# Query sets of one batch, key sets of two batches, and the last two query sets turned on GpSimd

## The chip, the cores and the metric

The kernel runs on one core of one Trainium2 chip. Its engines are TensorE (PE), VectorE (DVE), ScalarE (ACT), GpSimd (POOL) and SyncE (SP), which issues nearly all DMAs. The metric is the time of one execution on the device, in microseconds. The kernel before took 234.39 us (median of three runs, 233.6 to 234.4).

## The reference

One transformer block on x of 4 batches, 256 tokens, 512 features, in float32:

```
h  = layernorm(x)
q  = rope(h @ wq)   # 32 heads of 16
k  = rope(h @ wk)   # 8 key heads of 16, each serves 4 query heads
v  = h @ wv
a  = softmax(causal(q k^T / 4)) v
x  = x + layernorm(a @ wo)
z  = layernorm(x)
y  = z @ W_base^T + b + 16/16 * sum_e route_e(z) * B_e (A_e z)   # 8 experts, top 2
out = x + layernorm(y)
```

rope takes the pairs (re, im) of a head's features and gives re*cos - im*sin and re*sin + im*cos, with tables over the 256 positions.

## The kernel before

**Input.** Eight tiles of 128 tokens are loaded, normalised on DVE (`input_norm`), turned on PE (`turn_x`) and copied by ACT to `xn_t`, features on partitions (`copy_xnt`). SP issues the loads in program order (L298 to L314), and they travel in that order: x0, identity, wv, x1 to x3, half of wq, x4 to x7, tables, wk, the other half of wq, then the mask and the late weights.

**Projection sets.** Queries and keys are projected in float32 in five sets (L264): (half of the tokens, half of the heads) for queries, and one set "K" with all tokens. A set is 8 matmuls of 128x512 for queries. K is 16 matmuls of 64 columns of weights that run in pairs. Each set fills two PSUM banks, one for re and one for im.

**Rope and split.** Four products on DVE (L820), then the re half on DVE and the im half on POOL. Each half is split into three bf16 parts (high, middle, low) whose sum is the float32 value: ACT casts the high and middle parts (L606, L616), DVE (L831, L837) or POOL (L466, L470) subtract. The parts are written to DRAM (`write_q`, `write_k`) and loaded back (`load_q`, `load_k`), with heads apart and parts stacked on 96 partitions: one group is one batch and 4 key heads (16 query heads), and there are 8 groups. Queries lie in a ring of 5 slots `qst`, keys in a ring of 5 slots `kst`.

**The main loop.** There are 45 steps; unit n is one key head of one batch, 32 units in all. PE's step n does `scores(n)` (L1085, L1089; one bank), `scores_t(n-9)` (L1131), `scores_more(n)` (L1100, L1105; two banks), a piece of projection in steps 0 to 4 (L1036), `turn_max` at step 6, 10, ... (L1114) and, from step 14, a third of `attend` (L1146). DVE takes maxima of the scores (L964, L967), which frees their banks for the next step; every fourth step it splits the maxima in two bf16 parts (L977, L978). ACT copies the turned maxima (L726), SP stacks them under the queries (`stack_max`, L376), and `scores_t` then gives scores minus maximum, turned, which ACT exponentiates (L716, L719). POOL masks them (L543), and `attend` multiplies with the values. Sums and their inverses go through DRAM (`send_out`, `store_rden`, `spread_rden`).

**The fifth set** (i = 4) is the late one: 3 of its 8 matmuls run before the loop, 5 in steps 0 to 4. ACT copies its two banks to SBUF at step 5 (L746), POOL does the four products (L478) and both halves (L482), and `split_high`, `leave_late` (step 10), `split_middle`, `low_late` (step 12) and `write_q(4)` (step 14) follow. All engines work through their queues in program order, and every cross-engine dependence is a semaphore. After the loop the rest (output projection, layernorms, experts) runs in tiles of 128 tokens (`tile_step`), and the change doesn't touch it.

What must hold before the first scores is in `scores` and what PE runs before is in these lines:

```
            turn_and_project_v(0)
            project(0)
            turn_and_project_v(4)
            for i in range(1, 4):
                project(i)
            project(4, 0, 2 * KC - sum(MATMULS_4))
```

## Time and profile before

| what | us |
|---|---|
| median of three timed runs | 234.39 |
| the profiled execution's own time | 235.09 |
| its span, first to last instruction | 233.4 |
| PE busy (matmul) | 201.3 (86%) |
| DVE busy | 173.3 (74%) |
| ACT busy | 125.6 (54%) |
| POOL busy | 113.2 (49%) |

The span is cut into four stages below: until about 54.4 us the inputs are normalised and projected, from there the loop's steps 0 to 8 run until about 74.5, steps 9 to 13 until 88.8, and then PE is busy nearly all the time. A busy PE isn't a PE at its peak, since the ends of pipelined matmuls are modelled; idle time before an instruction and what ended it stand in brackets in the timeline.

### The profile page before, as it was taken

Reading aid. Unit: us, or ns where it says so; the run is one execution under the profiler, and the core shown is the slowest. Engines: PE = TensorE matmul, PEld = TensorE weight load, DVE = VectorE, ACT = ScalarE, POOL = GpSimd, SP = SyncE. Lnnn points to the kernel's source line nnn. Section 1 sums busy time; section 2 is a strip of 40 time slices with the busy share of each in tenths; the row PEclk is TensorE's granted clock in tenths of the full one; section 3 lists DMA queues with packets and bytes.
Section 4 is the critical chain, followed back from the end, with each engine's and each line's share of the span. In section 5 each row is a group of like instructions: output and inputs, shape, how many; then the busy total and the mean of one; then the engine's idle time right before and its main releaser. Section 6 shows DMA issues by size and latency. Waiting matters only on the chain.

```text
span 233.4 us, 3763 instructions
## 1 busy us (share of the span) xinstructions
PE 201.3 (86%) x1292; PEld 123.5 (53%) x1304; DVE 173.3 (74%) x364; ACT 125.6 (54%) x222; POOL 113.2 (49%) x96
## 2 busy tenths in 40 slices
PE   0499999999787879999999989899889989998860
PEld 0394843444454544444444524144778868997830
DVE  1773525767998897868696884686798898888785
ACT  3231440341214877888766785773577488773321
POOL 8200231562439695798743446462746262433352
PEclk9999999999999999999999999999999999999985
DMA  5998048976996302696673203344330001110113
GB/s 162 383 367 328 0 138 164 233 200 168 202 220 144 66 1 76 165 181 125 143 143 65 48 11 51 101 90 95 51 93 0 3 0 45 46 48 0 45 45 135
DMA packets 22465, 26.73 MB, mean 115 GB/s; under 512 B 3760, under 2 KB 17328, under 8 KB 21680
## 3 DMA queue, kind: packets, MB, share of 16 engines
q1 hardware_dynamic: 22304, 26.38, 44.8%
q8 instruction: 10, 0.16, 0.3%
q10 hardware_dynamic: 144, 0.13, 0.2%
q14 instruction: 7, 0.06, 0.1%
HBM read 17.19 MB, written 6.95 MB: 103 GB/s over the span
## 4 chain that ended last, share of the span: by engine, by line
PE 48%; DVE 22%; ACT 10%; issue 9%; DMA 5%; POOL 3%; SPq 2%; DVEq 0%; POOLq 0%
PE ps L1146 7%; PE ps L1194 7%; PE ps L1131 6%; PE ps L1105 4%; PE ps L1046 4%; PE ps L1169 4%; DVE stats L772 4%; PE ps L1036 3%; DVE nmax L967 3%; PE ps L1022 3%; DVE nmax L964 2%; ACT L577 2%; ACT region_a L719 2%; DMA x_sb<-x 2%; PE ps L1085 2%
## 5 line engine op out<-in xcount | busy, mean ns | idle before, releaser
L543 POOL TENSOR_SCALAR_AFFINE_SELECT region_a<-region_a 128x1024 f32<-128x1024 f32 x32 | 36.9, 1154 | 26.9 <-ACT region_a L719 26.7
L967 DVE TENSOR_REDUCE nmax<-ps 128x4 f32<-128x1024 f32 x32 | 39.1, 1223 | 10.3 <-PE ps L1105 10.0
L719 ACT ACTIVATE region_a<-ps 128x1024 f32<-128x1024 f32 x32 | 32.7, 1022 | 0.2 <-PE ps L1131 0.2
L1036 PE MATMUL ps<-region_a,region_c 128*128 128x512 f32 x64 | 29.0, 598 | 0.0
L1131 PE MATMUL ps<-region_b,kst 98*128 98x512 bf16 x96 | 26.8, 381 | 1.6 <-ACT region_a L719 1.1
L716 ACT ACTIVATE region_a<-ps 128x512 f32<-128x512 f32 x32 | 19.2, 599 | 16.4 <-PE ps L1131 15.9
L964 DVE TENSOR_REDUCE nmax<-ps 128x4 f32<-128x512 f32 x32 | 21.8, 682 | 4.8 <-PE ps L1089 4.4
L1146 PE MATMUL ps<-region_a,v_aug 128*32 128x512 f32 x192 | 25.3, 603 | 0.0
L583 ACT ACTIVATE std<-mv,eps_sb 128x1 f32<-128x1 f32 x32 | 9.3, 293 | 22.4 <-DVE mv L773 22.3
L1105 PE MATMUL ps<-kst,region_b 96*128 96x128 bf16 x256 | 19.6, 219 | 1.4 <-DVE nmax L967 0.8
L462 POOL TENSOR_TENSOR region_a<-region_a 128x512 f32<-128x512 f32 x4 | 6.5, 1627 | 28.9 <-DVE region_a L820 28.9
L1105 PEld LDWEIGHTS ps<-kst,region_b 96*128 96x128 bf16 x256 | 17.0, 98 | 5.5
L535 POOL TENSOR_TENSOR x_sb<-x_sb,region_b 128x512 f32<-128x512 f32 x8 | 10.2, 1278 | 18.9 <-ACT region_b L646 18.9
L530 POOL TENSOR_TENSOR region_b<-x_sb,region_b 128x512 f32<-128x512 f32 x7 | 9.0, 1281 | 19.4 <-ACT region_b L646 19.4
L1036 PEld LDWEIGHTS ps<-region_a,region_c 128*128 128x128 f32 x64 | 11.6, 190 | 12.8 <-issue 12.8
L820 DVE TENSOR_TENSOR region_a<-ps,region_c 128x512 f32<-128x512 f32 x16 | 9.9, 684 | 10.4 <-PE ps L1022 5.4
L772 DVE BATCH_NORM_STATS2 stats<-x_sb 128x6 f32<-128x512 f32 x16 | 11.0, 688 | 7.2 <-DMA x_sb<-x 6.1
L1194 PE MATMUL ps<-wcat_h,xn_h 128*128 128x324 f32 x64 | 11.6, 323 | 3.8 <-ACT xn_h L659 3.8
L577 ACT ACT_TABLE_LOAD x11 | 14.1, 1283 | 1.0 <-PEq L1290 0.8
L606 ACT CAST region_c<-region_a 128x512 bf16<-128x512 f32 x8 | 4.8, 618 | 18.3 <-DVE region_a L828 17.3
L1131 PEld LDWEIGHTS ps<-region_b,kst 98*128 98x128 bf16 x96 | 7.6, 97 | 12.3 <-ACT region_a L719 3.4
L1089 PE MATMUL ps<-kst,region_b 96*128 96x128 bf16 x128 | 12.4, 219 | 1.8 <-ACT mrow L726 0.8
(107 smaller groups left out, 415.3 us busy)
## 6 DMA issues: line engine op xcount, KB each, us to landing
q_scr<-region_c SPq DMA_DIRECT2D x24, 128.0 KB, 2.6
region_b<-q_scr SPq DMA_DIRECT2D x8, 384.0 KB, 5.2
x_sb<-x SPq DMA_DIRECT2D x8, 256.0 KB, 5.7
region_b<-q_scr SPq DMA_DIRECT2D x8, 256.0 KB, 5.6
attn_t<-o_sb SPq DMA_DIRECT2D x32, 64.0 KB, 2.4
rden_bc<-r_scr SPq DMA_DIRECT2D x8, 256.0 KB, 3.4
out<-region_b SPq DMA_DIRECT2D x7, 256.0 KB, 2.0
kst<-k_scr SPq DMA_DIRECT2D x8, 192.0 KB, 3.5
```

The lines of the kernel that those rows point to most:

```text
L543: pool.affine_select(out=blocks, in_=blocks, compare_op=ALU.is_ge, fill=0.0, base=0, pattern=[[0, 2], [0, REP], [1, P]], channel_multiplie ...
L577: nc.scalar.activation(unused[:, k, t:t + 1], eps_sb[:, 0:1], (ACT.Exp, ACT.Sqrt)[k])
L716: nc.scalar.activation(probs[:, u % PRING, 0, :], ps[:, 3, :], ACT.Exp, scale=float(HEAD_DIM) ** -0.5).then_inc(exp_done, 1)
L719: nc.scalar.activation(probs[:, u % PRING, 1:3, :], ps[:, 4:6, :], ACT.Exp, scale=float(HEAD_DIM) ** -0.5).then_inc(exp_done, 1)
L772: link(nc.vector.bn_stats(stats[:, k, t, :], src))
L964: nc.vector.tensor_reduce(nmax[:, gi % 2, 0, heads], ps[:, 0, :].rearrange("p (r k) -> p r k", r=REP), AX.X, ALU.max, negate=True).then_in ...
L967: nc.vector.tensor_reduce(nmax[:, gi % 2, 1, heads], ps[:, 1:3, :].rearrange("p a (r k) -> p r a k", r=REP), AX.XY, ALU.max, negate=True). ...
L1036: last = nc.tensor.matmul(ps[:, SET_BANKS[i][ri], :], wq_sb[:, c, col:col + P], xn_t[:, c, half * HALF:(half + 1) * HALF], start=(c == 0), ...
L1105: last = nc.tensor.matmul(ps[:, 1 + kt, r * P:(r + 1) * P], qst[0:SROWS, slot, h, P:2 * P], kst[0:SROWS, slot, k, kt * P:(kt + 1) * P], st ...
L1131: last = nc.tensor.matmul(ps[:, 3 + j, :], kst[0:TROWS, slot, k, kt * P:(kt + 1) * P], qst[0:TROWS, slot, k * REP:(k + 1) * REP, qt * P:(q ...
L1146: last = nc.tensor.matmul(ps[32 * j:32 * j + 32, 6 + qt, :], v_aug[:, 2 * b + kt, g * GROUP_KV + j, :], probs[:, u % PRING, qt + kt, :], s ...
L1194: last = nc.tensor.matmul(ps[:, 4 + 2 * (t % 2) + hf, 0:CATH], act_part[:, t % 2, c, :], w[:, c, hf * CATH:(hf + 1) * CATH], start=(term = ...
```

## The change

Query sets become one batch each with all 32 heads: 16 matmuls of 128x256. Key sets become two batches each: 16 matmuls of 64 columns by 256, in pairs. The six sets are q0, k01, q1, k23, q2, q3 (`SETS`). The first three are projected before the loop with their rope on DVE, both halves; k23 is projected last before the loop, and its rope is done on DVE in steps 0 to 3. Sets q2 and q3 are projected in steps 0 to 7, four matmuls in each, into banks 6 and 7; ACT copies them to SBUF (`LATE_COPY`), and POOL does all of their rope and subtractions (`LATE_ROTATE`, `LATE_HIGH`, `LATE_MIDDLE`). Before the loop POOL now does nothing but clear memory. The loads go x0, identity, x1, all of wq, x2, x3, tables, wk, x4 to x7, wv. Keys are written once for each part and repeated by the load (`load_k`, three DMAs with a broadcast source), and a ring of three whole batches holds them. The slots of `probs` are numbered from 3 (`slot_of`, `FIRST_SLOT`). The maxima's mask tile gives its place to `den_pk` and `rden_pk`, and `nmr` has two of four rows.

The diff, cut to its core ("..." marks what is left out):

```diff
-LOADS = {7: 4, 15: 5, 18: 6, 22: 7}
+LOADS_Q = {9: 4, 15: 5, 18: 6, 22: 7}
+LOADS_K = {8: 2, 18: 3}
 VECTOR_OUT = 5
@@ -69,10 +72,14 @@
 POWER_TILE = 5
-ROPE_3 = {0: 1, 1: 2}
-MATMULS_4 = (1, 1, 1, 1, 1)
-ROTATE_4, SPLIT_HIGH_4, SPLIT_MIDDLE_4, WRITE_4 = 5, 10, 12, 14
+LATE_PROJECT = 4
+K_ROPE = {0: 0, 1: 1, 2: 2, 3: 3}
+K_HIGH, K_MIDDLE = 2, 3
+LATE_COPY = {2: (2, 0), 4: (2, 1), 6: (3, 0), 8: (3, 1)}
+LATE_ROTATE = {2: 0, 8: 1}
+LATE_HIGH = {6: 4, 10: 5}
+LATE_MIDDLE = {7: 4, 12: 5}
+LATE_WRITE = {7: 2, 14: 3}
...
-        SETS = [(0, 0), "K", (0, 1), (1, 0), (1, 1)]
-        SET_BANKS = [(2, 3), (4, 5), (6, 7), (2, 3), (4, 5)]
-        set_of = {s: i for i, s in enumerate(SETS)}
-        WRITES_Q, WRITES_K = 16 * 2 * PARTS, 16 * 2 * len(RUNS)
-        LOADS_QK = 16 * (len(RUNS) + 1)
+        SETS = [("q", 0), ("k", 0), ("q", 1), ("k", 1), ("q", 2), ("q", 3)]
+        SET_BANKS = [(2, 3), (4, 5), (2, 3), (4, 5), (6, 7), (6, 7)]
+        DIRECT = 4
+        WRITES = 16 * 2 * PARTS
+        LOADS_OF_ONE = 16 * len(RUNS)
...
             sp.dma_start(ident_sb[:, :], ident).then_inc(ident_loaded, 16)
+            sp.dma_start(x_sb[:, 1, :], x[P:2 * P, :]).then_inc(x_loaded[1], 16)
+            sp.dma_start(wq_sb[:, :, :], wq.rearrange("(c p) n -> p c n", p=P)).then_inc(wq_loaded, 16)
+            for t in range(2, TILES):
+                sp.dma_start(x_sb[:, t, :], x[t * P:(t + 1) * P, :]).then_inc(x_loaded[t], 16)
+                if t == 3:
+                    sp.dma_start(tab_sb[:, :, :], tables).then_inc(tab_loaded, 16)
+                    sp.dma_start(wk_sb[:, :, :], wk.rearrange("(c p) n -> p c n", p=P)).then_inc(wk_loaded, 16)
             sp.dma_start(wv_sb[:, :, :], wv.rearrange("(c p) n -> p c n", p=P)).then_inc(wv_loaded, 16)
-            wq_v = wq.rearrange("(c p) n -> p c n", p=P)
-            for t in range(1, TILES):
-                if t == 4:
-                    sp.dma_start(wq_sb[:, :, 0:256], wq_v[:, :, 0:256]).then_inc(wq_loaded[0], 16)
-                sp.dma_start(x_sb[:, t, :], x[t * P:(t + 1) * P, :]).then_inc(x_loaded[t], 16)
-            sp.dma_start(tab_sb[:, :, :], tables).then_inc(tab_loaded, 16)
-            sp.dma_start(wk_sb[:, :, :], wk.rearrange("(c p) n -> p c n", p=P)).then_inc(wk_loaded, 16)
-            sp.dma_start(wq_sb[:, :, 256:512], wq_v[:, :, 256:512]).then_inc(wq_loaded[1], 16)
...
+            def load_k(b):
+                sp.wait_ge(k_written[b], WRITES)
+                if b >= KRING:
+                    sp.wait_ge(t_psum, 2 * KV_HEADS * (b - KRING + 1))
+                for part, (first, count) in enumerate(RUNS):
+                    rows = k_scr[b, part].rearrange("i f h n -> (i f) (h n)")
+                    sp.dma_start(kst[first * HEAD_DIM:(first + count) * HEAD_DIM, b % KRING, :, :],
+                                 rows.unsqueeze(0).broadcast_to([count, HEAD_DIM, KV_HEADS * SEQ]))\
+                        .then_inc(k_loaded[b % KRING], 16)
...
             write_q(0)
+            write_k(0, (0, 1))
             load_q(0)
+            write_k(0, (2,))
+            load_k(0)
+            load_q(1)
+            write_k(1, range(PARTS))
+            write_q(1)
+            load_k(1)
             load_q(2)
-            for part in range(PARTS):
-                for half in range(2):
-                    write_k(part, half)
-            load_k(0)
-            load_k(1)
-            write_q(2)
-            load_q(1)
-            load_k(2)
-            load_k(3)
             load_q(3)
-            write_q(3)
+            write_k(2, range(PARTS))
+            write_k(3, range(PARTS))
             for n in range(MAX_LAG, STEPS + 5):
...
+                if n in LATE_WRITE:
+                    write_q(LATE_WRITE[n])
+                if n in LOADS_K:
+                    load_k(LOADS_K[n])
+                if n in LOADS_Q:
+                    load_q(LOADS_Q[n])
...
+            def rotate_late(j):
+                cos, sin = (tab_sb[:, k, :].unsqueeze(1).broadcast_to([P, 2, SEQ]) for k in range(2))
+                re, im = (late_set[:, i, :].rearrange("p (g n) -> p g n", g=2) for i in range(2))
+                pool.wait_ge(tab_loaded, 16)
+                if j:
+                    pool.wait_ge(late_low, 2 * j)
+                for m, val, table in ((0, re, cos), (2, re, sin), (1, im, sin), (3, im, cos)):
+                    if m in (0, 1):
+                        pool.wait_ge(late_copied, 2 * j + m + 1)
+                    pool.tensor_tensor(late_mul[:, m, :].rearrange("p (g n) -> p g n", g=2), val, table, ALU.mult)\
                         .then_inc(late_multiplied, 1)
                 for i, op in enumerate((ALU.subtract, ALU.add)):
+                    pool.wait_ge(late_multiplied, 4 * j + 3 + i)
                     pool.tensor_tensor(late_rot[:, i, :], late_mul[:, 2 * i, :], late_mul[:, 2 * i + 1, :], op)\
                         .then_inc(late_rotated, 1)
...
+                if n in LATE_ROTATE:
+                    rotate_late(LATE_ROTATE[n])
+                if n in LATE_HIGH:
+                    leave_late(LATE_HIGH[n] - DIRECT)
+                if n in LATE_MIDDLE:
+                    low_late(LATE_MIDDLE[n] - DIRECT)
...
+            def copy_late(b, ri):
+                i = SETS.index(("q", b))
+                act.wait_ge(proj_psum, 2 * i + ri + 1)
+                if i > DIRECT:
+                    act.wait_ge(late_multiplied, 4 * (i - DIRECT))
+                else:
+                    act.wait_ge(proj_psum, 2 * DIRECT)
+                    act.wait_ge(v_psum, 2)
+                nc.scalar.copy(late_set[:, ri, :], ps[:, SET_BANKS[i][ri], :]).then_inc(late_copied, 1)
...
             sqrt(0, 0)
-            for t in range(1, 4):
+            sqrt(0, 1)
+            copy_xnt(0)
+            sqrt(0, 2)
+            copy_xnt(1)
+            for t in range(3, 6):
                 sqrt(0, t)
-                copy_xnt(t - 1)
-            sqrt(0, 4)
+            copy_xnt(2)
             copy_xnt(3)
-            for t in range(5, TILES):
-                sqrt(0, t)
+            split_high(0)
+            split_middle(0)
+            split_high(1)
+            split_middle(1)
+            sqrt(0, 6)
+            sqrt(0, 7)
             copy_v(0)
             for t in range(4, TILES):
                 copy_xnt(t)
-            split_high(0)
-            split_middle(0)
+            split_high(2)
+            split_middle(2)
             copy_v(1)
-            for i in range(1, 4):
-                split_high(i)
-                split_middle(i)
...
-                        act.wait_ge(proj_psum, len(SETS))
+                        act.wait_ge(part_l, 2 * DIRECT)
+                    if u == PRING - FIRST_SLOT:
+                        act.wait_ge(proj_psum, 2 * len(SETS))
...
+                if n == K_HIGH:
+                    split_high(3)
+                if n == K_MIDDLE:
+                    split_middle(3)
+                if n in LATE_COPY:
+                    copy_late(*LATE_COPY[n])
+                if n in LATE_HIGH:
+                    split_high(LATE_HIGH[n])
+                if n in LATE_MIDDLE:
+                    split_middle(LATE_MIDDLE[n])
...
+            def rope_multiply(i, ri):
+                a = i % 2
+                dve.wait_ge(proj_psum, 2 * i + ri + 1)
+                if i >= 2:
+                    dve.wait_ge(rotated, 2 * (i - 1))
+                if SETS[i][0] == "k":
+                    tables = [tab_sb[:, 2 + k, :] for k in range(2)]
+                    val = ps[:, SET_BANKS[i][ri], 0:SEQ]
+                    outs = [rope_t[:, a, m, 0:SEQ] for m in range(4)]
+                else:
+                    tables = [tab_sb[:, k, :].unsqueeze(1).broadcast_to([P, 2, SEQ]) for k in range(2)]
+                    val = ps[:, SET_BANKS[i][ri], :].rearrange("p (g n) -> p g n", g=2)
+                    outs = [rope_t[:, a, m, :].rearrange("p (g n) -> p g n", g=2) for m in range(4)]
+                for m, table in ((0, tables[0]), (2, tables[1])) if ri == 0 else ((1, tables[1]), (3, tables[0])):
+                    nc.vector.tensor_tensor(outs[m], val, table, ALU.mult).then_inc(rope_mul, 1)
...
+            input_tiles(0, 6)
+            dve.wait_ge(tab_loaded, 16)
+            for i in range(2):
+                rope_multiply(i, 0)
+                rope_multiply(i, 1)
+                for piece in (rope_add, rope_left, rope_low):
+                    piece(i, 0)
+                    piece(i, 1)
+            input_tiles(6, TILES)
...
+                if n in K_ROPE:
+                    for ri in range(2):
+                        (rope_multiply, rope_add, rope_left, rope_low)[K_ROPE[n]](3, ri)
...
+            def project_k(pair):
+                i = SETS.index(("k", pair))
+                pe.wait_ge(wk_loaded, 16)
+                pe.wait_ge(xnt_ready, 4 * pair + 4)
+                if i >= 2:
+                    pe.wait_ge(rope_mul, 4 * (i - 1))
+                for ri in range(2):
+                    for c in range(KC):
+                        for j in range(2):
+                            tokens = slice((2 * pair + j) * SEQ, (2 * pair + j + 1) * SEQ)
+                            last = nc.tensor.matmul(ps[64 * j:64 * j + 64, SET_BANKS[i][ri], 0:SEQ],
+                                                    wk_sb[:, c, 64 * ri:64 * ri + 64], xn_t[:, c, tokens],
+                                                    start=(c == 0), stop=(c == KC - 1))
+                    last.then_inc(proj_psum, 1)
+            def project_q(b, pieces=range(4)):
+                i = SETS.index(("q", b))
+                pe.wait_ge(wq_loaded, 16)
+                pe.wait_ge(xnt_ready, 2 * b + 2)
+                for piece in pieces:
+                    ri, g = divmod(piece, 2)
                     if i == 2:
+                        pe.wait_ge(rope_mul, 2 * ri + 2)
+                    if i == DIRECT:
                         pe.wait_ge(v_ready, 2)
-                    pe.wait_ge(xnt_ready, 4 * half + 4)
-                    for m in range(first, first + count):
-                        ri, c = divmod(m, KC)
-                        col = (2 * g + ri) * P
-                        last = nc.tensor.matmul(ps[:, SET_BANKS[i][ri], :], wq_sb[:, c, col:col + P],
-                                                xn_t[:, c, half * HALF:(half + 1) * HALF],
-                                                start=(c == 0), stop=(c == KC - 1))
-                if first + count == 2 * KC:
-                    last.then_inc(proj_psum, 1)
+                    if i > DIRECT:
+                        pe.wait_ge(late_copied, ri + 1)
+                    col = (2 * g + ri) * P
+                    for c in range(KC):
+                        last = nc.tensor.matmul(ps[:, SET_BANKS[i][ri], g * SEQ:(g + 1) * SEQ], wq_sb[:, c, col:col + P],
+                                                xn_t[:, c, b * SEQ:(b + 1) * SEQ], start=(c == 0), stop=(c == KC - 1))
+                    if g == 1:
+                        last.then_inc(proj_psum, 1)
...
+            turn_x(0)
+            turn_x(1)
+            project_q(0)
+            turn_x(2)
+            turn_x(3)
+            project_k(0)
+            for t in range(4):
+                project_v(t)
+            project_q(1)
+            for t in range(4, TILES):
+                turn_x(t)
+                if t > 4:
+                    project_v(t - 1)
+            project_v(TILES - 1)
+            project_k(1)
...
+                if n < 2 * LATE_PROJECT:
+                    project_q(2 + n // LATE_PROJECT, (n % LATE_PROJECT,))
...
```

## Rows read from the trace of the kernel before

**Rows 1.** The page's groups: DVE's rope products, busy us, mean ns, idle before them.
```profile
L820 DVE TENSOR_TENSOR region_a<-ps,region_c 128x512 f32<-128x512 f32 x16 | 9.9, 684 | 10.4 <-PE ps L1022 5.4
```
**Rows 2.** Windows, two stages: length, then busy us (instructions) by engine, PE clock, DMA.
```profile
54.40:74.50 20.10, 16.21 (x136) 9.62 (x138) 17.48 (x23) 5.09 (x8) 9.91 (x9) 1.00 0.81 169
...
88.80:141.00 52.20, 49.99 (x430) 22.77 (x429) 40.97 (x52) 40.93 (x65) 33.44 (x28) 1.00 0.51 107
```
**Rows 3.** Timeline, PE before the loop: start, length, line, tiles, count, idle before.
```profile
10.10 1.12 PE L1007 MATMUL ps<-ident_sb,region_b 128*128 128x128 f32 x4 [0.27 <-DVE region_b L786]
...
15.38 2.06 PE L1046 MATMUL ps<-region_c,region_a 128*128 128x128 f32 x16
17.28 7.03 PE L1036 MATMUL ps<-region_a,region_c 128*128 128x512 f32 x16
24.15 1.04 PE L1007 MATMUL ps<-ident_sb,region_b 128*128 128x128 f32 x8
...
30.23 7.09 PE L1022 MATMUL ps<-region_a,region_c 128*64 128x512 f32 x32
...
54.41 0.39 PE L1089 MATMUL ps<-kst,region_b 96*128 96x128 bf16 x4 [0.58 <-DMA kst<-k_scr]
```
**Rows 4.** First loads: an issue (timeline), landing times of one tile, of one tensor.
```profile
3.66 0.44 SPq L304 DMA_DIRECT2D region_c<-wq  x1
...
DMA to landing us min/median/max: 3.8/7.0/8.4
...
region_c<-wq SPq DMA_DIRECT2D x2, 512.0 KB, 7.2
```
**Rows 5.** Timeline, DVE and ACT, one input tile's statistics, normalisation and copy.
```profile
8.51 0.69 DVE L772 BATCH_NORM_STATS2 stats<-x_sb 128x6 f32<-128x512 f32 x1
...
9.50 0.55 DVE L786 TENSOR_SCALAR region_b<-x_sb,mv,rstd 128x512 f32<-128x512 f32 x1
...
11.25 0.59 ACT L588 COPY region_a<-ps 128x512 f32<-128x512 f32 x1 [0.61 <-PE ps L1007]
```
**Rows 6.** Timeline, PE in steps 4, 5, 6 and at the start of 15.
```profile
64.41 0.38 PE L1085 MATMUL ps<-mask_bf,ident_bf 128*128 128x512 bf16 x1
...
65.65 1.08 PE L1036 MATMUL ps<-region_a,region_c 128*128 128x512 f32 x2
66.57 0.38 PE L1085 MATMUL ps<-mask_bf,ident_bf 128*128 128x512 bf16 x1
...
70.07 0.29 PE L1114 MATMUL ps<-ident_bf,nmax_p 128*32 128x128 bf16 x2
...
89.64 0.39 PE L1085 MATMUL ps<-mask_bf,ident_bf 128*128 128x512 bf16 x1
```
**Rows 7.** Timeline, POOL: the late set's products, sums and last subtractions.
```profile
67.92 4.93 POOL L478 TENSOR_TENSOR attn_t<-region_c 128x512 f32<-128x512 f32 x4 [5.87 <-ACT region_c L746]
72.81 2.48 POOL L482 TENSOR_TENSOR attn_t<-attn_t 128x512 f32<-128x512 f32 x2
...
84.78 2.30 POOL L498 TENSOR_TENSOR region_c<-attn_t,region_c 128x512 bf16<-128x512 f32 x2
```
**Rows 8.** Timeline, ACT: first maxima, casts of the late set, sixth unit's exponentials.
```profile
70.39 0.36 ACT L726 COPY mrow<-ps 32x256 bf16<-32x256 bf16 x1 [2.55 <-PE ps L1114]
...
79.29 1.13 ACT L606 CAST region_c<-attn_t 128x512 bf16<-128x512 f32 x2
...
87.54 0.60 ACT L716 ACTIVATE region_a<-ps 128x512 f32<-128x512 f32 x1 [1.46 <-PE ps L1131]
88.03 1.02 ACT L719 ACTIVATE region_a<-ps 128x1024 f32<-128x1024 f32 x1
```
**Rows 9.** DVE's split of the maxima: ns min/median/max of eight, and the third.
```profile
L978 DVE TENSOR_TENSOR nmax_p<-nmax,nmax_p x8: 191/193/1032, 67.2 to 136.8; 128x32 bf16<-128x32 f32 x8
...
84.98 1.03 DVE L978 TENSOR_TENSOR nmax_p<-nmax,nmax_p 128x32 bf16<-128x32 f32 x1
```
**Rows 10.** The page's DMA issues: query loads of 48 rows, KB each, us to landing.
```profile
region_b<-q_scr SPq DMA_DIRECT2D x8, 384.0 KB, 5.2
```

More of the change, by code:

```diff
@@ L184, in build @@
         mask_loaded = sem("mask_loaded")
-        wq_loaded = [sem(f"wq_loaded{g}") for g in range(2)]
+        wq_loaded = sem("wq_loaded")
         tab_loaded = sem("tab_loaded")
@@ L330, in write_q @@
-                        sp.dma_start(dst[part, ri], parts[:, i % 2, ri, part, :].rearrange("p (b n) -> p b n", b=2))\
-                            .then_inc(scr_written[i], 16)
-            def write_k(part, half):
-                i = set_of["K"]
-                first, count = RUNS[part]
-                dst = k_scr[half].rearrange("(s i f) h n -> i (f h) s n", s=TERMS, i=2)
-                for ri in range(2):
-                    if part == 0:
-                        sp.wait_ge(part_h, 2 * i + 1 + ri)
-                    elif part == 1:
-                        sp.wait_ge(part_m, 2 * i + 1 + ri)
-                    else:
-                        sp.wait_ge(part_l[ri], i + 1)
-                    rows = parts[half * 64:half * 64 + 64, i % 2, ri, part:part + 1, :]
-                    sp.dma_start(dst[ri, :, first:first + count, :], rows.broadcast_to([64, count, HALF]))\
-                        .then_inc(k_written[half], 16)
@@ L791, in input_norm, with input_tiles @@
                 ln_apply(0, t, xn_sb[:, t, :], x_sb[:, t, :]).then_inc(xn_ready, 1)
-            for t in range(TILES):
-                dve.wait_ge(x_loaded[t], 16)
-                ln_stats(0, t, x_sb[:, t, :])
-                if t >= 1:
-                    input_norm(t - 1)
-            input_norm(TILES - 1)
+            def input_tiles(first, last):
+                for t in range(first, last):
+                    dve.wait_ge(x_loaded[t], 16)
+                    ln_stats(0, t, x_sb[:, t, :])
+                    if t > first:
+                        input_norm(t - 1)
+                input_norm(last - 1)
@@ L1050, in project_v, with keys @@
                     last.then_inc(v_psum, 1)
-            def turn_and_project_v(first):
-                for t in range(first, first + 4):
-                    turn_x(t)
-                    if t > first:
-                        project_v(t - 1)
-                project_v(first + 3)
-            turn_and_project_v(0)
-            project(0)
-            turn_and_project_v(4)
-            for i in range(1, 4):
-                project(i)
-            project(4, 0, 2 * KC - sum(MATMULS_4))
+            turn_x(0)
[13 more added lines that the diff above has]
+            project_k(1)
+            def keys(rows, gi, k, kt):
+                b, g = divmod(gi, 2)
+                return kst[0:rows, b % KRING, g * GROUP_KV + k, kt * P:(kt + 1) * P]
             def scores(n):
```

288 lines of the change are left out of this document (114 added, 174 removed).

## The prediction

> **What bounds the kernel now.** I read the profile from the coarse to the fine. The page's engine shares name PE (86% busy). Its groups show DVE's rope products at 0.68 us each with 10.4 us of idle time before them, most of it ended by PE [rows 1]: before the loop, DVE waits for PE. The windows by stage then say where PE itself has room. From 88.8 to 141 us it is busy 49.99 of 52.20 us, so a shift at its start is still there at the end. In the loop's first steps (54.4 to 74.5) PE is busy 16.21 of 20.10 us and DVE 17.48 [rows 2]. Room is only there and before the loop. So the change is worth the shift of one moment, the start of step 15 (89.64 before) [rows 6], unless a later wait is new; after step 15 I find none. Before the loop PE hardly stops, and the first scores waited 0.58 us for the keys' load, their mask matmul starting at about 54.2 [rows 3].
>
> **How long a set takes.** A query set is 8 matmuls of 512 columns in 7.03 us, 0.88 each. Two value tiles, 8 matmuls of 128 columns, took 2.06 with the last one's tail, so 0.95 for a tile and 0.24 for a matmul [rows 3]. On the line between the two, 256 columns take 0.45, and a new query set of 16 takes 7.2 us; half of 512 would make it 7.0. I take 7.1, since tails are counted in the small ones; the bounds cost 0.1 a set either way, 0.4 in all. Keys took 7.09 in all, so 3.6 each half. TensorE's work is thus about unchanged, only moved: before the loop stood 3 3/8 query sets, now 2, which is 9.6 us less.
>
> **The start of PE.** Tile x1 comes earlier (wv no longer ahead), but `turn_x(1)` needs DVE's normalisation of tile 1, and DVE queues that behind the statistics of tile 2, which is now behind all of wq. The bytes ahead of and in x2 are 256+64+256+1024+256 = 1,856 KB, the same as were in the queue to the end of wq's first half before. That half's landing follows from the rows: both halves have a median of 7.2, and the largest of the tile's is 8.4, so the first is 2*7.2-8.4 = 6.0 after its issue at 3.66, or 9.7 [rows 4]. From the start of statistics to the end of the normalisation of the tile before is 1.54 us (8.51 to 10.05) [rows 5]: `turn_x(1)` at 11.25 against 10.10. `project_q(0)` follows at once and needs its copy. Turn 10.10 to copy end 11.84 is 1.74 [rows 3, 5], so it starts at 13.1. Bounds for x2: 8.5 (wv's small rows are out of the way) and 10.5.
>
> PE starts slow. Four transposes took 1.12 us at 10.10, eight took 1.04 at 24.15 [rows 3]. From 10.10 to 17.28 it did three turns (0.45 each) and four value tiles (0.95 each), 5.15 us of work in 7.18. It lost 2.0 us, which is 4.1 us at half rate, between the levels of 1.2 and 2.4 GHz. The same 4.1 us from 11.25 end at 15.35, of which q0 gets 2.25 and loses 1.1. Bounds: 0 and 2.2. The Trainium skill's "TensorE: Matmul & The Clock Gate", Part 1, says that the engine is throttled by default and activity releases it. By that, the gaps before and after `turn_x(1)` could delay the release, and the sum would be up to 1.1 higher. The durations at 10.10 and 24.15 agree with it; what a gap does to the rise no row shows.
>
> Then: q0 13.1 to 21.3 (7.1+1.1); two turns and the wait for their copy 1.4 (24.15 plus turns, same shape), K01 at 22.7 to 26.3; four value tiles 3.8, to 30.1; q1 to 37.2; turns and values 4 to 7 as before, 24.15 to 30.23, 6.1, to 43.3; K23 to 46.9. **The first scores start at 46.9, 7.3 us earlier than 54.2.**
>
> **Is anything else late for 46.9?** Keys: before, from K's end in PSUM (37.3) to scores at 54.4 was 17.1 us with the products, splits, 12 writes and loads [rows 3]. The new set is there at 26.3 with half the columns, so even at the old price plus the query set ahead of it on SP it is there by 43.4. The second half of SP's order (12 + 6 writes, loads of 1 to 3) ends after q1's split, near 49; query loads land 5.2 us after issue [rows 10], near 54, and group 2 is wanted in step 8, beyond 70. 24 key writes for 12 and 12 key loads for 8 so cost nothing. Their cover is this slack, and without it each would cost its issue of about 0.5 us [rows 4]. DVE takes POOL's half of the rope, three subtractions or sums of a product's length in each set, about 2 us [rows 1], and is free for it, since it waits for PE there.
>
> **Steps 0 to 7.** A step with one late matmul took 2.16 us (64.41 to 66.57), 0.92 of it that matmul (65.65 to 66.57) [rows 6]. Four of 256 columns take 1.8 instead, so 3.05. DVE has 17.48 us in nine steps, 1.9 a step [rows 2]; k23's rope adds four products of half the 0.68 width [rows 1] in step 0, 1.4, and half of that in steps 1 to 3. That is 3.3 in step 0, 0.25 above PE's 3.05, and hidden in the rest; at full width it would be 2.7 and 1.4, and cost 1.6 in step 0. `turn_max` of step 6 starts, call it T, at 46.9 + 6*3.05 + 0.25 + 2.9 (scores 1.1, projection 1.8) = 68.4, against 70.07 [rows 6]: -1.7. So 5.6 of the 7.3 us have gone back into the steps, as they must: the work was only moved.
>
> **From T to step 15.** Before, that took 89.64-70.07 = 19.57 [rows 6]. Now step 7 has a projection (+1.8) and POOL has a second set to turn. ACT copies the maxima (ends T+0.7) [rows 6, 8], then, queued behind them, re of q3, then casts the high parts of q2 at 0.57 each [rows 8], to T+2.4. POOL: two subtractions of 1.15 to T+4.2, two more to T+6.5, four products 4.93 to T+11.4, two sums 2.48 to T+13.9 [rows 7]. Only then come the masks of units 0 to 3, and ACT's step 10 has `split_high(5)` between the exponentials of units 1 and 2. Before, it got there at T+9.2 (79.29) and found its data [rows 8]. Now it gets there at T+11 and leaves at T+14.5. Exponentials of a unit 1.5 [rows 8]: unit 2 to T+16.0; unit 3, whose last matmul needs unit 2's bank, to T+17.6; the middle cast waits for POOL (masks of 0 and 1, subtractions at T+17.3 and T+18.4) and ends T+19.0; unit 4 to T+20.5. Unit 5 was at T+17.5, so it comes 3.0 later, and PE, which needs unit 4's banks for unit 5, with it. POOL's mask of unit 3, for which `attend` waits, is done at T+20.6, just in time. **T to step 15 grows by 3.1 with the small waits of `attend`, and the sum is -1.7 + 3.1 = +1.4 us.** If the late data were ready, step 7's 1.8 alone would count, which is the lower bound; ACT's exponentials behind a POOL that is as slow in all ten as in its sums (1.24) would make it 3.6.
>
> DVE's split of the maxima, with two SBUF inputs, took 1.03 once, beside POOL's subtractions at 84.78, and 0.19 otherwise [rows 7, 9]. Step 8's will now lie beside POOL too: 0 to 0.84, and I take 0.2, as DVE has slack after step 7. "SBUF — State Buffer", "Who interferes with whom", of the Trainium skill has a DVE instruction with two SBUF inputs and a GpSimd one that reads SBUF exclude each other for a whole instruction; the trace agrees (1.03 beside 0.19), and by it the sum would be 0.84 instead of 0.2 here.
>
> The sum is +1.6 us: 236.7 against the profiled execution's own 235.09, 233.4 of it span. That one lies 0.7 above the median, so I predict **236.0** against 234.39.
>
> **The rivals.**
> 1. *ACT's and POOL's late work finds slack and only PE's step 7 counts.* For it: ACT had 1.46 us of slack before unit 5 [rows 8]. Against: ten POOL operations in a row between T+1.9 and T+13.9 have no gap. It gives -1.7+1.8 = +0.1: 234.5.
> 2. *Faster: the projections start early.* One mechanism, the start of PE: x2 lands at 8.5 (-1.2) and PE runs at its high rate through q0 (-1.1), so scores start at 44.6. For it: x1 and wq travel without the small rows of wv. Against: the slow turns at 10.10. With the late chain it gives 1.6-2.3 = -0.7, and with its stall gone (rival 1) -2.2: 232.2. It decides from a first score before about 45.3, and for 0.5% before 44.
> 3. *SP's queue.* Key and query loads of batch 2 now stand right before `stack_max(1)`; at 5.2 us to landing [rows 10] the second maxima may come after T+17, when step 13 wants them. Issue at T+12.7 and landing like the loads gives T+18: +1 to +2.5 on top, 237.5. Before, they were issued in a quiet queue.
> 4. *It doesn't do what it says*, keys still gate the first scores, as they did [rows 3]: each us past 46.9 counts whole. Three us late is 239. Against it, the slack of 3.5 us above.
>
> **How the numbers follow.** Forecast 0.40, rival 1 0.25, rival 2 0.19, rival 3 0.12, rival 4 0.04. No change is within 0.5%, 1.2 us. The forecast's own range, 234.5 to 237.5, lies mostly above 235.6: slower 0.32 of its 0.40, plus 0.14 of rivals 3 and 4, 0.46. Same: 0.08, rival 1's 0.22 and a few of rival 2, 0.32. Faster: 0.22. The range is 232.8 to 238.2, to rival 2's far end and past rival 3.
>
> **What would show it.** First scores near 46.9; `turn_x(1)` near 11.25; steps of 3.05 until step 7; POOL without a gap from T+1.9 to T+14; an idle ACT before step 10's high cast; step 15 at about 91.2. If the first scores start before 45, or ACT doesn't stop in step 10, the forecast is wrong.

## The result: slower by 6.9%, and the profile after

The changed kernel takes 251.31 us (median of 4 runs, 248.62 to 252.76) against 234.39. The ratio is 1.0692, 95% interval 1.0600 to 1.0784. The forecast was 236.0, and 238.2 the upper end of its range. The profiled execution took 250.75 us, with a span of 249.0. Medians here and below are over all runs and ratios over those in the chip's faster state, and where one run was slow the median without it is 250.75 for the changed kernel, 239.50 for the first experiment, 245.06 for the third and 233.55 for the one with repeated writes.

TensorE's timeline before and in the loop (start, length, line, tiles, count, idle before) shows where the forecast holds and where it breaks:

```profile
11.05 1.12 PE L1037 MATMUL ps<-ident_sb,region_b 128*128 128x128 f32 x4 [1.36 <-DVE region_b L794]
12.94 8.83 PE L1075 MATMUL ps<-region_a,region_c 128*128 128x256 f32 x32 [0.77 <-ACT region_a L581]
...
43.74 3.67 PE L1052 MATMUL ps<-region_a,region_c 128*64 128x256 f32 x32
51.82 0.59 PE L1129 MATMUL ps<-mask_bf,ident_bf 128*128 128x512 bf16 x1 [4.41 <-issue]
...
53.90 3.64 PE L1075 MATMUL ps<-region_a,region_c 128*128 128x256 f32 x8
57.38 0.38 PE L1129 MATMUL ps<-mask_bf,ident_bf 128*128 128x512 bf16 x1
...
58.48 1.95 PE L1075 MATMUL ps<-region_a,region_c 128*128 128x256 f32 x8
60.27 0.38 PE L1129 MATMUL ps<-mask_bf,ident_bf 128*128 128x512 bf16 x1
```

`turn_x(1)` is at 11.05 (forecast 11.25), and the last keys leave TensorE at 47.4 (43.74 + 3.67; forecast 46.9), with the first query set 0.6 us longer than forecast. Then it waits 4.41 us, and the first scores start at 51.82 instead of 46.9. The row names no releaser for this wait ("issue"); that it was for batch 0's keys is shown by the second experiment below, which changes their load alone. Their step's projection takes 3.64 us, those of later steps 1.95: a step is 2.89 us (57.38 to 60.27), under the forecast's 3.05.

The windows (length, busy us by engine, granted clock, DMA share, GB/s) of both waits, of this one and of a later one:

```profile
47.20:50.00 2.80, 0.21 (x2) 0.00 (x0) 0.00 (x0) 0.00 (x0) 0.00 (x0) 1.00 0.99 209
50.00:52.00 2.00, 0.18 (x1) 0.14 (x2) 0.00 (x0) 0.00 (x0) 0.00 (x0) 0.62 0.78 239
52.00:54.00 2.00, 2.00 (x15) 1.53 (x13) 0.69 (x1) 0.00 (x0) 0.00 (x0) 0.50 0.45 135
54.00:56.00 2.00, 2.00 (x7) 1.64 (x6) 1.85 (x4) 0.00 (x0) 0.00 (x0) 0.50 0.13 39
56.00:58.00 2.00, 2.00 (x10) 1.30 (x10) 0.69 (x3) 0.00 (x0) 0.00 (x0) 0.67 0.35 71
...
91.00:92.00 1.00, 1.00 (x6) 0.50 (x7) 0.00 (x0) 0.79 (x2) 1.00 (x1) 0.73 0.20 75
92.00:93.00 1.00, 1.00 (x9) 0.76 (x8) 0.15 (x1) 1.00 (x2) 1.00 (x2) 0.50 0.16 62
93.00:94.00 1.00, 0.67 (x5) 0.36 (x3) 1.00 (x2) 0.74 (x2) 1.00 (x2) 0.50 0.12 49
94.00:95.00 1.00, 0.00 (x0) 0.00 (x0) 0.97 (x3) 0.00 (x0) 1.00 (x2) 0.50 0.13 42
```

From 47.4 to 50 TensorE has run out and nothing else computes, while the DMA engines are 99% busy, so this stretch alone doesn't show idle DMA engines. The clock then falls to 0.50, the 1.2 GHz level, and stays there until after 56. The second wait is odd in another way: from 92 to 95 us traffic still flows, at 42 to 62 GB/s, with a DMA share of 0.12 to 0.16. The share is a mean over 16 engines, so two or three engines' worth is at work. The key and query loads behind which this wait stands were issued by SyncE some ten microseconds earlier (its queue: start, length, line, tensors, count):

```profile
39.98 2.06 SPq L374 DMA_DIRECT2D kst<-k_scr  x3
42.10 1.34 SPq L364 DMA_DIRECT2D region_b<-q_scr  x3
43.48 3.69 SPq L352 DMA_DIRECT2D k_scr<-region_c  x6
47.21 4.45 SPq L342 DMA_DIRECT2D q_scr<-region_c  x6
54.82 1.95 SPq L374 DMA_DIRECT2D kst<-k_scr  x3
...
81.75 1.94 SPq L374 DMA_DIRECT2D kst<-k_scr  x3
83.80 1.28 SPq L364 DMA_DIRECT2D region_b<-q_scr  x3
85.13 18.70 SPq L381 DMA_DIRECT2D region_b<-mrow  x4
```

Key loads (`kst<-k_scr`) come first, then query loads (`region_b<-q_scr`), then `stack_max(1)` (`region_b<-mrow`). The last, small as it is (8 KB), lands late. The chain that ended last has it, and it has the query loads behind the next batch's key loads (start, length, step):

```profile
85.73 10.33 DMA region_b<-mrow
...
117.77 11.04 DMA region_b<-q_scr
```

TensorE waited for it in step 13, and before that, in its step 12, for the exponentials that stood in ACT's step 10 behind the high cast:

```profile
90.03 0.39 PE L1178 MATMUL ps<-region_b,kst 98*128 98x512 bf16 x1 [2.51 <-ACT region_a L723]
...
96.11 1.46 PE L1178 MATMUL ps<-region_b,kst 98*128 98x512 bf16 x3 [2.44 <-DMA region_b<-mrow]
...
103.06 0.39 PE L1129 MATMUL ps<-mask_bf,ident_bf 128*128 128x512 bf16 x1
```

The last row is step 15, before at 89.64 [rows 6]. The table follows TensorE through the landmarks; "split" is the first experiment below, which differs in nothing but how the keys are loaded.

| us | before | forecast | after | split |
|---|---|---|---|---|
| first scores | 54.2 | 46.9 | 51.8 | 48.3 |
| T (`turn_max`, step 6) | 70.07 | 68.4 | 75.01 | 68.97 |
| step 15 | 89.64 | 91.1 | 103.06 | 94.06 |
| span | 233.4 | 235.0 | 249.0 | 237.8 |

(The forecast's span is 233.4 + 1.6. For split the trace has no record of the first mask matmul, and 48.3 is the next row's 48.52 less the 0.2 that one takes.) Each column is one execution, and they differ before any edit acts: the first query set took 8.83 us in "after" and 10.05 in "split", with the same instructions up to there. Against the forecast, 6.6 us are lost before T, 5.4 between T and step 15 (28.05 instead of 22.7), and 2.0 behind it, where the forecast had nothing. 1.21 of these are the wait for the query load of 11.04 us:

```profile
128.86 0.39 PE L1129 MATMUL ps<-mask_bf,ident_bf 128*128 128x512 bf16 x1 [1.21 <-DMA region_b<-q_scr]
```

### The profile page after: what moved, and what is told of

Read it like the earlier page. It is cut to its first block, busy times and chain, and to the rows that moved or that the text cites. A ratio compares the mean times of both kernels' runs of the same rounds, so it can differ in the third digit from the quotient of the medians.

```text
span 249.0 us, 4012 instructions
## 1 busy us (share of the span) xinstructions
PE 208.9 (84%) x1400; PEld 141.5 (57%) x1400; DVE 178.6 (72%) x376; ACT 128.3 (52%) x228; POOL 111.4 (45%) x94
## 2 busy tenths in 40 slices
DMA packets 19399, 25.97 MB, mean 104 GB/s; under 512 B 3892, under 2 KB 13364, under 8 KB 18612
## 4 chain that ended last, share of the span: by engine, by line
PE 21%; DVE 15%; DMA 12%; ACT 8%; issue 5%; SPq 4%; POOL 1%; DVEq 0%; POOLq 0%
DMA region_b<-mrow 6%; PE ps L1244 5%; DMA region_b<-q_scr 4%; PE ps L1178 4%; PE ps L1196 4%; DVE stats L780 4%; PE ps L1219 2%; ACT L570 2%; ACT region_a L726 2%; DMA r_scr<-mask_f 2%; PE ps L1152 2%; SPq L374 1%; DVE gate L914 1%; DVE xn_l L958 1%; DVE gate L906 1%
## 5 line engine op out<-in xcount | busy, mean ns | idle before, releaser
L536 POOL TENSOR_SCALAR_AFFINE_SELECT region_a<-region_a 128x1024 f32<-128x1024 f32 x32 | 38.3, 1204 | 27.6 <-ACT region_a L726 27.3
L471 POOL TENSOR_TENSOR attn_t<-region_c 128x512 f32<-128x512 f32 x8 | 10.1, 1290 | 56.2 <-ACT region_c L624 56.0
L1178 PE MATMUL ps<-region_b,kst 98*128 98x512 bf16 x96 | 28.5, 397 | 7.7 <-DMA region_b<-mrow 3.0
L1075 PE MATMUL ps<-region_a,region_c 128*128 128x256 f32 x128 | 33.2, 414 | 0.8 <-ACT region_a L581 0.8
L1075 PEld LDWEIGHTS ps<-region_a,region_c 128*128 128x128 f32 x128 | 25.9, 209 | 4.8 <-issue 1.1
L723 ACT ACTIVATE region_a<-ps 128x512 f32<-128x512 f32 x32 | 19.2, 599 | 16.7 <-PE ps L1178 16.2
L1152 PEld LDWEIGHTS ps<-kst,region_b 96*128 96x128 bf16 x256 | 18.5, 103 | 6.8 <-issue 1.6
L1152 PE MATMUL ps<-kst,region_b 96*128 96x128 bf16 x256 | 21.1, 229 | 0.0
L1129 PE MATMUL ps<-mask_bf,ident_bf 128*128 128x512 bf16 x32 | 13.0, 407 | 7.0 <-issue 4.4
L1129 PEld LDWEIGHTS ps<-mask_bf,ident_bf 128*128 128x128 bf16 x32 | 3.2, 102 | 19.6 <-issue 16.3
L581 ACT COPY region_a<-ps 128x512 f32<-128x512 f32 x8 | 4.5, 587 | 18.4 <-PE ps L1037 18.4
```

Source lines behind the costliest of these rows:

```text
L536: pool.affine_select(out=blocks, in_=blocks, compare_op=ALU.is_ge, fill=0.0, base=0, pattern=[[0, 2], [0, REP], [1, P]], channel_multiplie ...
L723: nc.scalar.activation(probs[:, slot_of(u), 0, :], ps[:, 3, :], ACT.Exp, scale=float(HEAD_DIM) ** -0.5).then_inc(exp_done, 1)
L1075: last = nc.tensor.matmul(ps[:, SET_BANKS[i][ri], g * SEQ:(g + 1) * SEQ], wq_sb[:, c, col:col + P], xn_t[:, c, b * SEQ:(b + 1) * SEQ], sta ...
L1152: last = nc.tensor.matmul(ps[:, 1 + kt, r * P:(r + 1) * P], qst[0:SROWS, slot, h, P:2 * P], keys(SROWS, gi, k, kt), start=(kt == 0), stop= ...
L1178: last = nc.tensor.matmul(ps[:, 3 + j, :], keys(TROWS, gi, k, kt), qst[0:TROWS, slot, k * REP:(k + 1) * REP, qt * P:(qt + 1) * P], start=T ...
```

## The experiments

Medians are of the runs on one chip together; before took 234.08 us beside the first four kernels, 234.02 beside the next three and 234.46 beside the last two. Ratios are to before. The changed kernel's 251.31 stands beside 234.39. Differences between kernels of different groups hold to some tenths of a microsecond at best.

### Key loads without a leading repetition

In the changed kernel each of a batch's three key loads reads the 16 rows of its part once per copy: its source begins with a dimension of stride zero, 3, 2 or 1 long. Here each copy is a DMA of its own.

```
-  sp.dma_start(kst[first * HEAD_DIM:(first + count) * HEAD_DIM, ...],
-      rows.unsqueeze(0).broadcast_to([count, HEAD_DIM, KV_HEADS * SEQ]))
+  for copy in range(first, first + count):
+      sp.dma_start(kst[copy * HEAD_DIM:(copy + 1) * HEAD_DIM, ...], rows)
```

> The changed kernel, its key load of each part given as one DMA per copy (six of 16 rows) in place of three DMAs whose source is repeated by a leading broadcast of 3, 2 and 1. Theory A (a load with a leading broadcast of 3 or 2 copies moves over few of the 16 DMA engines, holds those engines' rings for about 10 us, and everything queued behind it on them lands late): first scores go from 51.8 us to 47.3, the granted clock stays at 1.00 in steps 0 to 13, the stacked maxima land in 2 to 3 us instead of 10.3, and the time is 235 to 237.5 us, the forecast with nothing else wrong. Rival B (the order and volume of SP's queue are at fault, key and query loads side by side before the stacked maxima): the bytes are the same and three more issues are added for each batch, so landings stay long and the time stays at 248 to 253. Rival C (the late set's POOL work is what costs): only the wait before the first scores goes, 243 to 246.

Measured: 239.56 us, ratio 1.0201 [1.0156, 1.0246], 11.8 under the changed kernel. Rivals B and C fell, but so did part of theory A: the time is 2.1 us above its range of 235 to 237.5, and the clock does not stay at 1.00. Twice the key loads carry the same bytes (25.98 MB in all, without the edit 25.97). The page has:

```profile
region_b<-q_scr SPq DMA_DIRECT2D x8, 384.0 KB, 4.8
...
region_b<-q_scr SPq DMA_DIRECT2D x8, 256.0 KB, 5.4
...
kst<-k_scr SPq DMA_DIRECT2D x24, 64.0 KB, 2.2
```

The changed kernel's page has 6.3 and 6.9 us for the two kinds of query load. mrow's slowest landing falls from 10.3 to 5.3 us. TensorE never waits for it, nor (beyond 0.16 us) before the first scores:

```profile
48.52 0.39 PE L1133 MATMUL ps<-kst,region_b 96*128 96x128 bf16 x4 [0.16 <-issue]
```

So the waits were the loads' shape, neither their bytes nor their number.

### The same, for batch 0's keys alone

```
+  if b == 0:
+      for copy in range(first, first + count): ...   # one DMA a copy
+      continue
```

> The changed kernel with one DMA per copy for batch 0's keys alone; batches 1 to 3 keep the broadcast. It divides the loss between the first wait and the later ones. Theory A: first scores at 47.3 with a fast first step, 6 us gained, and the later waits for stacked maxima (2.4 us at step 13) and for a query load (1.2) stay: 243 to 246. Rival B: no gain, 250 to 252. A third reading, that only the first wait matters: 235 to 238.

Measured: 245.17, ratio 1.0446 [1.0396, 1.0495]. The first scores start at 47.2, so the wait before the loop is gone, worth about 6 us with the half clock behind it (251.31 - 245.17 is 6.1). The second wait stays, since batch 2's load is as it was. In the traces split loads everywhere save 5.7 us more of the span (243.5 against 237.8): 3.0 from T to step 15 (28.08 against 25.09) and 3.8 behind it, where TensorE waited 1.7 us for a query load, less 1.1 by which this execution had come to T sooner:

```profile
89.11 1.46 PE L1183 MATMUL ps<-region_b,kst 98*128 98x512 bf16 x3 [2.52 <-DMA region_b<-mrow]
```

### The kernel before, with such loads

Keys are written once and loaded with a leading repetition, by groups, in the kernel before; all else is untouched.

```
-  sp.dma_start(kst[0:SROWS, gi % RING, :, :], k_scr[b // 2, ...])
+  for part, (first, count) in enumerate(RUNS):
+      sp.dma_start(kst[first * HEAD_DIM:(first + count) * HEAD_DIM, ...],
+          rows.unsqueeze(0).broadcast_to([count, HEAD_DIM, GROUP_KV * SEQ]))
```

> The kernel before, with only its keys' way through DRAM changed: each part is written once and loaded by three DMAs with a leading broadcast of 3, 2 and 1 copies, per group. Sets, order, late work and clock-relevant work stay. Theory A: first scores 3 to 8 us later than 54.2 us, some loads and stacked maxima landing in 7 to 11 us; time 238 to 250. Rivals B and C, by which the broadcast is harmless: within 1 us of 234.4, or a little faster as a third fewer key bytes are written.

Measured: 245.78, ratio 1.0500 [1.0452, 1.0548]. The time is in theory A's range, but two of its signs missed: the first scores came at 54.0, no later than before's 54.2, and mrow's slowest landing is 4.6 us, not 7 to 11. The loss came by the waits below, in a program without any of the changed kernel's other parts. For the 2.8 us on mrow the trace shows a second way to be late: SyncE took 7.92 us to issue six query writes (before 4.30), and so issued mrow at 73.80, 1.6 us after it was ready. Why it took so long no run shows; with plain copies, in the next run, it took 3.12. (Waits of TensorE: for what, us in total, times, longest):

```profile
PE ps L1087 <- DMA region_b<-q_scr: 3.2, 2, 1.6
PE ps L1133 <- DMA region_b<-mrow: 2.8, 1, 2.8
...
PE ps L1091 <- DMA kst<-k_scr: 1.8, 1, 1.8
```

### The kernel before, with six small loads

```
+      for copy in range(first, first + count):
+          sp.dma_start(kst[copy * HEAD_DIM:(copy + 1) * HEAD_DIM, ...], rows)
```

> The kernel before, keys written once and loaded by six DMAs of 16 rows per group with no broadcast: the control of the run before this one, with more issues than it. Theory A: within 2 us of 234.4, since each DMA has 16 rows to spread. If it is the number of DMAs or of SP's issues that hurts, it is slower than the broadcast form, 240 or more.

Measured: 240.30, ratio 1.0282 [1.0244, 1.0320]. It beats the repetition by 5.5 us, but the expectation failed: small loads aren't free there. SyncE issues twelve in a row for two groups, 5.88 us, and the writes and loads of the next queries stand behind them (SyncE's queue, then TensorE in step 4):

```profile
48.04 5.88 SPq L372 DMA_DIRECT2D kst<-k_scr  x12
53.96 4.35 SPq L330 DMA_DIRECT2D q_scr<-region_c  x6
```

```profile
66.16 0.41 PE L1087 MATMUL ps<-mask_bf,ident_bf 128*128 128x512 bf16 x1 [3.11 <-DMA region_b<-q_scr]
```

0.49 us an issue is the 0.5 that the prediction took, and here there is no slack for it. Over the kernel before, more issues and the other form of the writes together cost 6.2 us; the repetition, with half as many issues, costs 5.5 more (4.8 from 245.06). In the changed kernel the loads are by batch, so that six issues serve two groups.

### The high cast earlier

Without the loads' cost 239.56 is left, 3.6 above the forecast. What stands out in the trace of split loads is ACT's stop in step 10, which the forecast had, TensorE's stall for it in step 12, and the clock behind it (windows as above):

```profile
84.03 0.61 PE L1178 MATMUL ps<-region_b,kst 98*128 98x512 bf16 x1 [2.53 <-ACT region_a L723]
```

```profile
84.00:91.00 7.00, 6.19 (x29) 3.31 (x29) 3.68 (x5) 5.04 (x7) 7.00 (x7) 0.55 0.00 1
```

```
-LATE_HIGH = {6: 4, 10: 5}
-LATE_MIDDLE = {7: 4, 12: 5}
+LATE_HIGH = {5: 4, 10: 5}
+LATE_MIDDLE = {6: 4, 12: 5}
```

> The run with one DMA per key copy, and the fourth set's high cast one step earlier (step 5 in place of 6, ahead of the first maxima's copy on ACT) and its middle cast at step 6 in place of 7. Theory A2 (what is left of the loss is POOL's chain that reaches ACT's step 10 late, and the half clock that PE gets after waiting for it): the second rotation starts about 3.4 us earlier, the cast in step 10 finds its data, the 2.5 us wait of PE at step 12 goes, the clock stays at 1.00 and step 15 comes 19.6 to 21.5 us after the first turn of the maxima in place of 25.1; time 235 to 237 us. Rival D (the eight steps with projection make the loss, the chain is only beside it): within 0.7 us of 239.6. Rival E (the first projection's slow start is the larger part): 238 to 239.

Measured: 235.81, ratio 1.0079 [1.0048, 1.0110]: 3.8 us less by the medians and 2.9 by the ratios, for a stall of 2.5. In the traces T to step 15 falls from 25.09 to 21.70 us (70.75 to 92.45), by 3.4, just past the 21.5 expected, and the granted clock stays at 1.00 in it. The first late set is cast a step earlier, POOL gets through both sets in time, and in the profile after it TensorE's waits for L723 come to 0.4 us in place of 3.0.

### A busy TensorE ahead of its first work

```
+  idle_turns(10)      # identity times identity into bank 2, which the first set overwrites
   turn_x(0)
+  idle_turns(4)
   turn_x(1)
+  idle_turns(3)
   project_q(0)
```

> The run before this one in the list, plus 17 matmuls of the identity with itself before and between the first two turns and ahead of the first projection (results are overwritten and not used). Theory: the first query set takes 7.1 us in place of 8.8 to 10.1, first scores start 1.5 to 3 us earlier, and the time is 1.5 to 3 us under the run without them, 232.5 to 235. Rival: PE's speed there does not depend on what PE did before, or the first scores wait for the keys' way through DRAM as soon as PE comes earlier: no change.

> The kernel before with 10 matmuls of the identity with itself ahead of its first turn: the control for the run before, since a kernel that gains by this should be compared with one that has it too. The first turns and value tiles lost 2.0 us to the slow rate: 232.4 if all of it counts, 234 if the keys' way through DRAM, for which the first scores waited 0.6 us, or the input tiles' arrival take its place. I expect 233.5.

Measured: 233.46, ratio 0.9984 [0.9963, 1.0005], 2.35 under the kernel without them; and ten such matmuls ahead of before's first turn give 232.97, ratio 0.9972 [0.9943, 1.0001]. The first query set falls to what the prediction took for a set at full rate, 7.1:

```profile
14.03 7.14 PE L1079 MATMUL ps<-region_a,region_c 128*128 128x256 f32 x32
```

It was 8.83 in the changed kernel and 10.05 with split loads, on the same 32 matmuls; over five executions without the idle ones, all with the same code up to there, it lay between 8.64 and 10.16. The set starts no sooner for them (14.03 against 12.94), it is only shorter. With its loads, its casts and its start mended, the changed kernel is 0.5 us (233.46 - 232.97) above the kernel before with the same start: the rearrangement itself buys nothing that these runs can tell.

### Repeated in the write, one load a batch

```
-  sp.dma_start(k_scr[b, part, ri]..., parts[rows, i % 2, ri, part, 0:SEQ])
+  sp.dma_start(dst[ri, :, first:first + count, :],
+      parts[rows, i % 2, ri, part:part + 1, 0:SEQ].broadcast_to([64, count, SEQ]))
...
-  for part, (first, count) in enumerate(RUNS): ...   # six loads a batch
+  sp.dma_start(kst[0:SROWS, b % KRING, :, :], k_scr[b])
```

> e6_warm with one thing changed: each part of a batch's keys is written to scratch repeated, by a DMA whose source has the repetition, and each batch's 96 rows are loaded by one DMA of 96 rows without a leading repetition, so that SyncE issues one load a batch in place of six. Theory (the loads hurt only because a leading repetition of three leaves them on three DMA engines, and not by their number): the time stays at e6_warm's 233.46 or comes up to 0.7 us below it, 232.8 to 233.6, since the five issues saved per batch stood in slack on SyncE, and mrow's slowest landing stays at 6 us or under. Rival (the repeated source of the writes is itself slow, or the three times larger write lands late): the first scores start later than in e6_warm by 1 us or more, and the time is 234.5 or above.

The base is the kernel with all three mendings (split loads, early cast, busy start). Measured: 233.57, ratio 0.9966 [0.9942, 0.9990], beside that one's 0.9984; the rival, 234.5 or above, didn't come. A repetition that stands behind the 64 partitions, in the write, and not ahead of the rows in the load, costs nothing here. The page has the loads of 96 rows at

```profile
kst<-k_scr SPq DMA_DIRECT2D x4, 384.0 KB, 3.7
```

### The early cast alone, with the slow loads

The changed kernel with the two lines of the early cast and nothing else (the high and middle cast of the first late set one step earlier).

> The changed kernel as it is, its key loads with the repetition of three in the source included, with only the high and the middle cast of the later sets put two or more steps earlier (LATE_HIGH {5:4, 10:5}, LATE_MIDDLE {6:4, 12:5}). It tells whether the two costs add. If the 3.8 us that the same edit gave with split loads (239.56 to 235.81) add to the loads' 11.8: 247.5. If, as I think, the landing of mrow behind the slow key loads (10.3 us, waited for by step 13) is reached sooner by the steps that the edit makes faster, and so takes part of it back: 249 to 251, with the wait for region_b<-mrow longer than the 2.44 us of the changed kernel.

Measured: 249.68, ratio 1.0681 [1.0625, 1.0736]. The edit that gave 3.8 us with split loads gives 1.6 here by the medians and 0.3 by the ratios, and the intervals overlap: no gain that these few runs can tell. The traces show a smaller gain too: T to step 15 is 27.0 us (74.53 to 101.54) in place of 28.05, a gain of 1.0 where it was 3.4. ACT no longer stops in step 10, and step 13 still waits for mrow:

```profile
94.45 1.46 PE L1178 MATMUL ps<-region_b,kst 98*128 98x512 bf16 x3 [2.45 <-DMA region_b<-mrow]
```

The wait is as long as without the edit (2.44), not longer, as I had written, and its end came only 1.66 us sooner. SyncE's queue and the chain say what sets that end:

```profile
80.07 1.94 SPq L374 DMA_DIRECT2D kst<-k_scr  x3
...
87.36 14.95 SPq L381 DMA_DIRECT2D region_b<-mrow  x4
```

```profile
87.96 6.44 DMA region_b<-mrow
```

mrow was issued 2.2 us later than in the changed kernel (87.96 against 85.73) and landed 1.7 us sooner (94.40 against 96.06). The key loads ahead of it were issued 1.68 us sooner (80.07 against 81.75). From their first issue to mrow's landing it is 14.33 us here, 14.31 there, and 14.42 where batch 0's loads alone are split (74.64 to 89.06): the landing follows the key loads, with the query loads right behind them, and not its own issue. A faster step shortens nothing in it but the start.

## Why the prediction was wrong, step by step

- **The step that failed** is the sentence "24 key writes for 12 and 12 key loads for 8 so cost nothing. Their cover is this slack". It priced the loads by their bytes and issues, at the landing of a load of another shape (and from it had 3.5 us of slack). The keys were issued in time, at 39.98, but the first scores came 11.8 us later, where before's loads landed in 3.5. A load with a leading repetition of three leaves most DMA engines idle: share 0.12 to 0.20 at 42 to 75 GB/s from 91 to 95 us. Against the same bytes in separate loads it costs 11.8 us (251.31 to 239.56), and in the kernel before 5.5 (245.78 to 240.30). The slack was also summed wrong: 43.4 is 26.3 + 17.1 and leaves out the query set that the sentence says it has. That is not what failed.
- The Trainium skill's "DMA: Bandwidth & Descriptors" has the rule, in "Rules for kernel authors": a leading zero-stride repetition of a few copies keeps a DMA to at most that many engines. The share of two or three engines out of 16 from 92 to 95 us agrees. The prediction did not weigh this rule, though it is the one that speaks against the change.
- **Rival 4** named the place, with a chance of 0.04: keys gate the first scores. They came 4.9 us late, of which 0.5 was TensorE's. Its "each us past 46.9 counts whole" was too little: TensorE had waited 4.41 us and worked at 0.50 until after 56, and the first projection took 3.64 instead of 1.95. From the first scores to T it took 23.2 us, and 20.7 with split loads: the half clock cost 2.5. Less the 0.8 that the shorter steps gave back (below), these with the 4.9 are the 6.6 that T is late.
- **Rival 3** named the second place, with the right queue and the wrong reason: `stack_max(1)` came late not since it stood behind loads of 5.2 us, but since the loads ahead of it had the leading repetition (its slowest landing 10.3; 5.3 with split loads, where step 13 doesn't wait). The prediction made rivals 3 and 4 exclude each other, where one cause brings both.
- **Right:** `turn_x(1)`, 11.05 for 11.25; the end of the projections, 47.4 for 46.9; that DVE hides the keys' rope; T to the end of ACT's casts. POOL's second products start at T+6.4 (forecast 6.5) and its sums end at T+13.8 (13.9), and ACT's cast ends at T+14.5 (14.5):

```profile
81.45 4.94 POOL L471 TENSOR_TENSOR attn_t<-region_c 128x512 f32<-128x512 f32 x4
86.34 2.49 POOL L475 TENSOR_TENSOR attn_t<-attn_t 128x512 f32<-128x512 f32 x2
```

```profile
87.65 0.62 ACT L601 CAST region_c<-attn_t 128x512 bf16<-128x512 f32 x1 [2.62 <-POOL attn_t L475]
88.86 0.62 ACT L601 CAST region_c<-attn_t 128x512 bf16<-128x512 f32 x1 [0.60 <-POOL attn_t L475]
```

- **Right place, wrong size:** T to step 15 grew by 5.5 us with split loads (94.06 - 68.97 = 25.09 against 19.57), not by 3.1. The stall alone was 2.53, and behind it TensorE ran 7 us at 0.55. The half clock was in no term of the sum. So the loads alone don't account for the miss: with them mended 239.56 is still above the range's 238.2. The 0.2 for DVE's split in step 8 came to nothing (0.19 us at 81.39); the slow one, 1.20 at 69.47, was the first, beside POOL's sums.
- **The start:** forecast a loss of 1.1 on the first query set; it was 1.7 in the changed kernel (8.83 against 7.14) and 2.9 with split loads, though no edit acts before it in either.
- **A step** of one projection was taken as 3.05 and measured 2.89; from the first scores to T that gave 0.8 back (20.7 for 21.5). So with split loads T is only 0.6 later than forecast, though the scores started 1.4 late.

The sum of the three mendings is 251.31 - 11.75 - 3.75 - 2.35 = 233.46. They add in this order only: while the first is not made, the second is worth 1.6 by the medians, 1.0 in the traces and 0.3 by the ratios.

## What to carry to other kernels

Price a DMA by its access pattern before its bytes: a repetition that leads the pattern can keep most of the 16 engines out of the transfer (share 0.12 to 0.16 here), and a small transfer that many wait for must not stand behind it. Put the repetition behind the partitions, or write the copies out where SyncE has room for the issues (in the kernel before it hadn't). Price a stall of TensorE at more than its length: after waits of 2.5 and 4.4 us it worked at half clock for 5 to 7 us, which cost about another 0.9 (3.4 regained in the trace for a stall of 2.5) and 2.5 (first scores to T, 23.2 against 20.7). When two landmarks are late by one mechanism, its chance is one number and its price the sum.

## What the runs showed of the hardware

- A transfer of 8 KB took 10.33 us to land behind three key loads, the first issued 4.0 us before it (81.75 and 85.73), against a median of 2.1.
- The granted clock does not show the slow start. In the changed kernel's window from 13 to 22 us it reads 1.00 with TensorE busy throughout, and yet the first query set took 8.83 us there, and 7.14 after 17 idle matmuls, where the same window reads 1.00 too:

```profile
13.00:22.00 9.00, 9.00 (x36) 7.67 (x37) 4.94 (x13) 0.59 (x2) 0.00 (x0) 1.00 1.06 378
```

- 32 matmuls of 256 columns in fp32 take 7.14 us, 16 of 512 columns 7.03 [rows 3]: the split by batch costs TensorE 0.1 a set.
- One DVE normalisation took 2.73 us beside POOL's memset of kst, and 0.55 at 10.45. The first turn waited for it, but the first query set waits for `turn_x(1)` at 11.05:

```profile
5.73 2.73 DVE L794 TENSOR_SCALAR region_b<-x_sb,mv,rstd 128x512 f32<-128x512 f32 x1
```

```profile
2.97 5.21 POOL L458 MEMSET kst<- 2x6144 bf16 x1
```
